# The last expert stored tile by tile, the final sum in the experts' block, and the first expert rows loaded inside the attention block

## The reference, cut to what matters

```python
x = x + 0.5 * ffn0(layernorm(x))      # 8 experts, top 2, capacity counted per expert
x = x + attention0(layernorm(x))      # 16 heads of 8, keys from a strided convolution
x = x + 0.5 * ffn0(layernorm(x))
x = x + 0.5 * ffn1(layernorm(x))      # causal attention inside, then 16 experts, top 2
x = x + attention1(layernorm(x))      # causal, 16 heads of 8
x = x + 0.5 * ffn1(layernorm(x))

# the experts of ffn1, after its own attention and layer norm (xt)
m1, m2 = one_hot(top1), one_hot(top2)           # of 16 experts
m1 = m1 * (loc1 < C); m2 = m2 * (loc2 < C)      # C = 512 rows an expert
xin  = einsum('tec,td->ecd', dispatch, xt)      # rows sent to the experts
h    = gelu(xin @ fc1_w + fc1_b)                # 128 -> 512
eout = (h @ fc2_w + fc2_b) * 0.8                # 512 -> 128
out  = resid + einsum('tec,ecd->td', combine, eout)
```

## Time and profile before

| | |
|---|---|
| median of 3 runs | 1950.85 us |
| lowest, highest | 1948.93, 1954.16 us |
| the profiled execution: its own time | 1948.95 us |
| its span, first to last instruction | 1947.2 us |
| PE busy | 1548.6 us (80%) |
| DVE busy | 1297.8 us (67%) |
| ACT busy | 966.4 us (50%) |
| POOL busy | 1078.7 us (55%) |
| mean granted clock of TensorE | 0.879 |
| HBM read, written | 104.34, 80.74 MB |

### The profile page before, as it was taken

How to read it: one execution, slowest core, us unless ns; L and a number is a source line. 1 busy time by engine, 2 the same in 40 slices (tenths; PEclk the granted TensorE clock), 3 DMA queues, 4 the chain that set the end, 5 groups by cost and what they waited for, 6 DMA issues and landing times. The chain is left out here.

```text
span 1947.2 us, 46256 instructions
## 1 busy us (share of the span) xinstructions
PE 1548.6 (80%) x17646; PEld 941.7 (48%) x17646; DVE 1297.8 (67%) x3322; ACT 966.4 (50%) x2039; POOL 1078.7 (55%) x1712
## 2 busy tenths in 40 slices
PE   5648788876599999854798599999999999744993
PEld 4532333345255555433576355555555555423772
DVE  7348888782688878734421688888888887544324
ACT  4215667732166677520233166777777776411331
POOL 3447766505378775545355376555757765552552
PEclk9977999977599999865799599999999999755996
DMA  8443322204333223100343442332323322001445
GB/s 288 112 131 104 90 82 80 75 23 123 114 120 104 82 88 99 42 28 23 114 138 98 138 126 84 92 100 78 113 84 98 97 81 83 26 23 56 141 130 156
DMA packets 233185, 188.08 MB, mean 97 GB/s; under 512 B 30044, under 2 KB 221368, under 8 KB 232326
## 3 DMA queue, kind: packets, MB, share of 16 engines
q1 hardware_dynamic: 222582, 166.36, 28.5%
q0 software_dynamic: 10240, 18.76, 2.9%
q10 hardware_dynamic: 144, 0.00, 0.0%
HBM read 104.34 MB, written 80.74 MB: 95 GB/s over the span
## 5 line engine op out<-in xcount | busy, mean ns | idle before, releaser
L1008 DVE TENSOR_REDUCE mx<-PS 128x2 f32<-128x512 f32 (+3 forms) x1408 | 784.2, 612 | 189.0 <-PE PS L648 137.5
L858 ACT ACTIVATE pt<-PS 128x512 f32<-128x512 f32 (+2 forms) x1408 | 667.6, 537 | 312.1 <-PE PS L648 227.6
L665 PE MATMUL PS<-ka,qa 52*128 52x256 bf16 (+3 forms) x2048 | 461.7, 305 | 65.2 <-DVE mx L1008 47.4
L781 PE MATMUL PS<-qa,ka 55*128 55x512 bf16 (+3 forms) x1792 | 459.7, 321 | 41.3 <-DMA qa<-nm 17.8
L725 PE MATMUL PS<-pt,vs 128*32 128x512 f32 (+3 forms) x3584 | 349.6, 481 | 2.3 <-issue 1.5
L648 PE MATMUL PS<-mask_q,identh 64*128 64x64 bf16 x3072 | 299.5, 193 | 1.5 <-issue 1.4
L648 PE MATMUL PS<-mask_k,identh 64*128 64x64 bf16 x3072 | 299.0, 192 | 0.9 <-issue 0.9
L781 PEld LDWEIGHTS PS<-qa,ka 55*128 55x128 bf16 x1792 | 166.9, 94 | 273.7 <-issue 119.3
L648 PEld LDWEIGHTS PS<-mask_k,identh 64*128 64x128 bf16 x3072 | 249.2, 97 | 51.7 <-issue 6.8
L648 PEld LDWEIGHTS PS<-mask_q,identh 64*128 64x128 bf16 x3072 | 252.4, 98 | 31.0 <-issue 8.9
L1161 POOL CAST nm<-nm 16x128 bf16<-16x128 f32 x128 | 36.2, 283 | 340.1 <-ACT nm L890 329.3
(11 more groups left out here) (249 smaller groups left out, 2333.4 us busy)
## 6 DMA issues: line engine op xcount, KB each, us to landing
pt<-in_f_w SPq DMA_DIRECT2D x96, 256.0 KB
qa<-q_parts SPq DMA_DIRECT2D x256, 96.0 KB, 2.3
ka<-k_parts SPq DMA_DIRECT2D x192, 96.0 KB, 2.3
q_parts<-parts SPq DMA_DIRECT2D x32, 384.0 KB, 3.4
k_parts<-parts SPq DMA_DIRECT2D x24, 384.0 KB, 2.6
xn<-y_rows SPq DMA_DIRECT2D x32, 256.0 KB, 3.2
hid<-y_rows SPq DMA_DIRECT2D x32, 256.0 KB, 3.7
q_parts<-parts SPq DMA_DIRECT2D x32, 256.0 KB, 3.2
```

The costliest lines, as they stand in the source:

```text
L665: mm = pe.matmul(PS[:, bank, i * n:(i + 1) * n], k.qa[rows, b % 2, g, h // 2, qb * P:(qb + 1) * P], k.ka[rows, b % 2, g, h // 2, 0:n], sta ...
L781: mm = pe.matmul(PS[:, bank, i * n:(i + 1) * n], k.ka[rows, b % 2, g, h // 2, kb * P:(kb + 1) * P], k.qa[rows, b % 2, g, h // 2, q0:S], st ...
L858: nc.scalar.activation(k.pt[:, u % 2, at[c]:at[c] + len(heads) * n], PS[:, SC_BANK + c % RING, 0:len(heads) * n], ACT.Exp, scale=SCORE_SCA ...
L1008: nc.vector.tensor_reduce(out, PS[:, MX_BANK + t % RING, 0:len(heads) * n] .rearrange("p (h n) -> p h n", n=n), AX.X, ALU.max).then_inc(s. ...
```

## The change

There are three parts. First, the last expert of every experts stage is done tile by tile: TensorE waits for all four activations, runs the chunks inside the tile loop with a PSUM bank for each tile, and signals after each tile; VectorE adds the bias tile by tile; POOL waits for each tile before it sends it. Second, the last `experts1` call is given the output: its own block goes on with all sixteen loads of results, the sum and the stores, and the separate last block is gone. Third, in the attention blocks whose rows are sent, SP waits at the end for the probabilities, the marks' sum and all sent rows, and then issues the loads of rows of experts 0 to 2 and of weights of experts 0 and 1, which before were the first thing that SP did in the experts' block. `AHEAD` (3, as before) becomes a constant, and `load_weights` and `load_rows` become functions outside `moe`.

```diff
--- before.py
+++ after.py
@@ -66,6 +66,7 @@
 ROOT_STEPS = ((0.703952253, 2.38924456), (0.5, 3.0))
 XT_BANK, H_BANK, Y_BANK = 0, 2, 6
 INV_BANK = 5
+AHEAD = 3
 FIRST_PHASES = ((0, 16), (16, 32))
 PHASES = ((0, 20), (20, 28), (28, 32))
 SENT_PHASES = ((0, 8), (8, 16), (16, 28), (28, 32))
@@ -1322,6 +1323,16 @@
             if not r.sent:
                 for i in range(B - 3, B):
                     store_rows(sp, k, i)
+            else:
+                sp.wait_ge(*s.pv_done.at(U))
+                sp.wait_ge(*s.inv_full.at(1))
+                sp.wait_ge(*s.first_sent.at(16 * NT))
+                for j, (first, end) in enumerate(r.phases):
+                    sp.wait_ge(*s.second_sent[j].at(16 * (end - first)))
+                for e in range(AHEAD):
+                    load_rows(sp, k, r, e)
+                    if e < 2:
+                        load_weights(sp, k, front, e)
 
     counts = {
         s.ln_step: k.entry_steps, s.pl_step: k.pool_steps, s.st_ready: len(ENTRY_GROUPS), s.mo_ready: NB - B, s.fm_ready: B - 2,
@@ -1343,7 +1354,22 @@
         signal.base += n
 
 
-def moe(nc, k, r, src, dst, gate_scale, renorm, src_scale):
+def load_weights(sp, k, w, e):
+
+    s, par = k.sig, e % 2
+    sp.dma_start(k.w1[:, par, :], w.w1[e * C:(e + 1) * C, :]).then_inc(s.w1_landed[par].h, 16)
+    sp.dma_start(k.w2[:, par, :, :], w.w2[e * FH:(e + 1) * FH, :].rearrange("(f p) c -> p f c", p=P))\
+        .then_inc(s.w2_landed[par].h, 16)
+
+
+def load_rows(sp, k, r, e):
+
+    ring, capacity = e % RING_E, r.w.capacity
+    sp.dma_start(k.xe[ring][:, :, :], k.xe_rows[e * capacity:(e + 1) * capacity, :]
+                 .rearrange("(t p) c -> p t c", p=P)).then_inc(k.sig.xe_loaded[ring].h, 16)
+
+
+def moe(nc, k, r, src, dst, gate_scale, renorm, src_scale, final=None):
 
 
     s, PS, w, E, capacity = k.sig, k.PS, r.w, r.E, r.w.capacity
@@ -1358,7 +1384,7 @@
 
         return ap.unsqueeze(2).to_broadcast([P, NT, E])
 
-    AHEAD = RING_E - 1
+    LAST_BANKS = (Y_BANK + (E - 1) % 2, XT_BANK, Y_BANK + E % 2, XT_BANK + 1)
     landed, landings = (s.xe_loaded, 16) if r.sent else (s.xe_landed, 16 * ST)
 
     with nc.Block() as block:
@@ -1399,12 +1425,27 @@
                                        k.w2[:, par, f, :], start=(f == 0 and t == 0), stop=(f == FC - 1 and t == ST - 1))
                 mm.then_inc(s.y_full.h, 1)
 
+            def last_output():
+
+                par = (E - 1) % 2
+                pe.wait_ge(*s.w2_landed[par].at(16 * PAIRS))
+                pe.wait_ge(*s.y_ready.at(E - 2))
+                pe.wait_ge(*s.act_done.at(E * FC))
+                for t in range(ST):
+                    if t == 2:
+                        pe.wait_ge(*s.y_ready.at(E - 1))
+                    for f in range(FC):
+                        mm = pe.matmul(PS[:, LAST_BANKS[t], 0:C], k.hT[:, par, f, t * P:(t + 1) * P],
+                                       k.w2[:, par, f, :], start=(f == 0), stop=(f == FC - 1))
+                    mm.then_inc(s.y_full.h, 1)
+
             rows_T(0)
             for e in range(E):
                 hidden(e)
                 if e + 1 < E:
                     rows_T(e + 1)
-                output(e)
+                    output(e)
+            last_output()
 
         @block.scalar
         def _(act):
@@ -1489,6 +1530,14 @@
                 nc.vector.tensor_tensor(k.ys[ring][:, 0:ST, :], PS[:, Y_BANK + e % 2, 0:capacity]
                                         .rearrange("p (t c) -> p t c", c=C), b2, ALU.add).then_inc(s.y_ready.h, 1)
 
+            def last_result():
+                ring = (E - 1) % RING_E
+                dve.wait_ge(*s.y_stored[ring].at(16 * ST * (E // RING_E - 1)))
+                for t in range(ST):
+                    dve.wait_ge(*s.y_full.at(E + t))
+                    nc.vector.tensor_tensor(k.ys[ring][:, t, :], PS[:, LAST_BANKS[t], 0:C], w.b2[:, (E - 1) * C:E * C],
+                                            ALU.add).then_inc(s.y_ready.h, 1)
+
             differences()
             rows(0)
             shares()
@@ -1501,8 +1550,12 @@
                     gates()
                 elif src_scale and e <= NG:
                     scale_source(e - 1)
-            result(E - 1)
+            last_result()
             k.route_steps = link.n
+            if final is not None:
+                for i in range(B):
+                    for c in range(2):
+                        combine(nc, k, dve, dst, i, c)
 
 
 
@@ -1518,9 +1571,10 @@
 
             def deliver(e):
 
-                pool.wait_ge(*s.y_ready.at(e + 1))
                 for t in range(ST):
                     n = e * ST + t
+                    if t == 0 or e == E - 1:
+                        pool.wait_ge(*s.y_ready.at(e + 1 + t))
                     pool.indirect_dma_start(k.y_rows[:, :], bass.IndirectOffsetOnAxis(k.idx[:, 1, n:n + 1], 0),
                                             k.ys[e % RING_E][:, t, :], None).then_inc(s.y_stored[e % RING_E].h, 16)
 
@@ -1537,42 +1591,32 @@
 
         @block.sync
         def _(sp):
-            def load_weights(j, par):
-                e = 2 * j + par
-                if not (isinstance(j, int) and j < 1):
+            for e in range(E):
+                if e >= 2:
                     sp.wait_ge(*s.y_full.at(e - 1))
-                sp.dma_start(k.w1[:, par, :], w.w1[bass.ds(e * C, C), :]).then_inc(s.w1_landed[par].h, 16)
-                sp.dma_start(k.w2[:, par, :, :], w.w2[bass.ds(e * FH, FH), :].rearrange("(f p) c -> p f c", p=P))\
-                    .then_inc(s.w2_landed[par].h, 16)
-
-            def fetch_sent(e):
-                ring = e % RING_E
-                if e == 0:
-                    sp.wait_ge(*s.first_sent.at(0))
-                    for signal in s.second_sent:
-                        sp.wait_ge(*signal.at(0))
-                if e > AHEAD:
-                    sp.wait_ge(*s.eT_full.at(e - AHEAD))
-                sp.dma_start(k.xe[ring][:, :, :], k.xe_rows[e * capacity:(e + 1) * capacity, :]
-                             .rearrange("(t p) c -> p t c", p=P)).then_inc(s.xe_loaded[ring].h, 16)
-
-            if r.sent:
-                for e in range(AHEAD):
-                    fetch_sent(e)
-                    if e < 2:
-                        load_weights(e // 2, e % 2)
-            for e in range(E):
                 if not (r.sent and e < 2):
-                    load_weights(e // 2, e % 2)
+                    load_weights(sp, k, w, e)
                 if r.sent and e + AHEAD < E:
-                    fetch_sent(e + AHEAD)
+                    if e >= 1:
+                        sp.wait_ge(*s.eT_full.at(e))
+                    load_rows(sp, k, r, e + AHEAD)
             for ring in range(RING_E):
                 sp.wait_ge(*s.y_stored[ring].at(16 * ST * (E // RING_E)))
-            load_results(sp, k, 0)
+            if final is None:
+                load_results(sp, k, 0)
+            else:
+                out, stored = final
+                for i in range(B):
+                    load_results(sp, k, i)
+                for i in range(B):
+                    sp.wait_ge(*s.combined.at(2 * i + 2))
+                    sp.dma_start(out[i].rearrange("(t p) c -> p t c", p=P),
+                                 dst[:, i * S:(i + 1) * S].rearrange("p (t c) -> p t c", c=C)).then_inc(stored, 16)
+                sp.wait_ge(stored, 16 * B)
 
     counts = {
         s.diff_ready: 2, s.exp_ready: 2, s.rt_step: k.route_steps, s.eT_full: E, s.eT_free: E,
-        s.h_full: FC * E, s.act_done: FC * E, s.y_full: E, s.y_ready: E,
+        s.h_full: FC * E, s.act_done: FC * E, s.y_full: E + ST - 1, s.y_ready: E + ST - 1,
     }
     for group in (s.w1_landed, s.w2_landed):
         counts |= {x: 16 * PAIRS for x in group}
@@ -1967,8 +2011,8 @@
         def experts0(r):
             moe(nc, k, r, x, x, 0.5, ("add", 1e-9), 0.0)
 
-        def experts1(r):
-            moe(nc, k, r, hid, x, 0.5 * 0.8, ("max", 1.1920929e-07), 0.5)
+        def experts1(r, final=None):
+            moe(nc, k, r, hid, x, 0.5 * 0.8, ("max", 1.1920929e-07), 0.5, final)
 
         entry0 = Segment(attn0, x, x, False)
         entry1, entry1f = Segment(attn1, x, x, True), Segment(attn1f, x, hid, True, twice=True)
@@ -1980,24 +2024,7 @@
         attention(nc, k, [entry1f], route1)
         experts1(route1)
         attention(nc, k, [entry1, entry1f], route1)
-        experts1(route1)
-
-        with nc.Block() as block:
-            @block.vector
-            def _(dve):
-                for i in range(B):
-                    for c in range(2):
-                        combine(nc, k, dve, x, i, c)
-
-            @block.sync
-            def _(sp):
-                for i in range(1, B):
-                    load_results(sp, k, i)
-                for i in range(B):
-                    sp.wait_ge(*k.sig.combined.at(2 * i + 2))
-                    sp.dma_start(out[i].rearrange("(t p) c -> p t c", p=P),
```

(3 more changed lines are left out.)

## The result

The changed kernel takes 1940.06 us, median of 5 runs (1936.86 to 1941.49), against 1950.85 us (1948.93 to 1954.97, 5 runs) for the kernel before on the same chip: ratio 0.994 [0.992, 0.996], 10.8 us less. The profiled execution took 1940.06 us (span 1938.3, granted clock 0.884), 8.9 us less than the 1948.95 us profiled before.

The account below looks back on a forecast made before the run. It took the kernel to be bound by one core's dependent order, where all engines wait. Gains 0.8 + 4.7 + 1.95 + 3.9 = 11.35 us gave 1937.6 from the profile, 1939.5 from the median; forecast 1938.5, range 1934.5 to 1944.

Parts of the forecast that it names:

- early loads: Experts' entries of the third and fourth stages: rows loaded inside the attention block start TensorE 2.35 us earlier, 4.7 us together.
- final block: Final sum after the last sends: sixteen loads in a row, no barrier; gain 3.9 us, of which 1.95 is the tile order.
- tile order: Last expert of each stage: POOL sends earlier, 1.95 us per 512-row stage, 0.8 together for the 256-row stages.
- The clock keeps its time: Rival at the experts' entries: TensorE's clock rises at 1796.7 regardless, giving back 1.2 us each; 1940.9 us, chance 0.20.
- tile four is full at 1914.3 and added by 1914.6, well before POOL wants it: Last 512-row stage: tiles take TensorE 0.93 us each, so adds stay hidden behind POOL's 1.27 us a tile; gain 1.95 us.
- the price of the first tile: 256-row stages: first tile's matmuls start 0.1 us after the last activation and take 0.93; POOL sends 0.4 us earlier.
- The bound of 1.4 us for both short stages: Stages of 256 rows: tile order gains 0.8 us together, between 0 and 1.4, POOL's idle time there.
- the stall allowed for: Final sum: one added stall of 0.4 us, the second piece landing 2.6 us after the first against 2.24 of work.
- Pieces come slowly: Rival at the final sum: each piece lands 2.6 us after the last, 2.1 us back; 1940.6 us, chance 0.10.
- The rows are not there: Rival at the experts' entries: sends count as landed only with POOL's DRAIN; 6.8 us lost, 1945.3 us, chance 0.08.
- Slower: Rival at three attention entrances: low clock lasts 13 us longer, costing 6.5 us each; 1958 us, chance 0.03.
- The terms named for the range's lower end: Below the forecast: 0.8 barrier at its bound, 0.4 no stall, 1.0 profiled run's level, 1.6 earlier clock rise; to 1934.5.

Follow-up runs that it names:

- chip Z: Chip of the last four follow-up kernels: kernel before 1951.03 us, changed kernel run again word for word 1943.50 us, ratio 0.996.
- fillers: Changed kernel plus 14 unused f32 matmuls on TensorE, after the last sent rows land in the attention block, chip Z: 1940.96 us, ratio 0.995 to the kernel before.
- chip Y: Chip of three tile loop shapes and the changed kernel with four early issues (1858.49 us, ratio 0.994); kernel before 1867.93 us there.
- taking issues away: Changed kernel with four early load issues instead of seven, and chunk waits, chip Z: 1940.85 us, ratio 0.994 to the kernel before.
- X: Chip of the moved wait and of the three parts each run alone; kernel before 1949.29 us there.
- the moved wait: Changed kernel with TensorE's wait before the last expert's third tile moved ahead of the first, chip X: 1942.65 us, ratio 0.996 to the kernel before.
- three loop shapes: Changed kernel with tiles three and four alternating, a wait per hidden chunk, or one signal after tile four, chip Y: 1858.34, 1858.36 and 1868.72 us.
- chunk waits: Changed kernel with a wait per hidden chunk in the last expert, not one for all four: 1858.36 us on Y; with four early issues on Z, 1940.85.

## Why the prediction was right

The forecast was 1938.5 us, range 1934.5 to 1944.0; measured 1940.06, and 1943.50 on chip Z. Total and sign came out. The early loads and the final block did what they were forecast to do; the tile order, two terms of the sum, did not, so it is partly luck that the total is this close.

- **Early loads: 4.7 us forecast, right in place and size.** At the six entrances profiled without early loads the restart lies 6.65 to 6.88 us after the marks, mean 6.79; at the eight with all seven issues early and no fillers, outside chip Y, 4.09 to 4.74, mean 4.38. That is 2.41 us each, forecast 2.35. SP is last at the barrier by the DRAIN lines, and taking issues away moved the barrier by 0.54 and 0.64. SP's first load came 0.07 to 0.69 us after the marks (forecast 0.25). In the third stage SP's DRAIN ends only 0.17 us behind POOL's in the first profile, in the fourth 0.8. Alone the part gave 4.2 us.
- **"The clock keeps its time" (0.20): did not happen.** In the first profiles it seemed to: the third stage's clock rose 7.0 us after the restart instead of 4.9, and that entrance gave back 1.05 us; the fourth gained 0.32. But the stretch from first to second transposes is 6.96 to 8.40 us, mean 7.79, at the six unchanged entrances, and 7.52 to 8.01, mean 7.71, at the ten early ones without fillers outside chip Y. What looked like a price was scatter. The rise itself came 4.9 to 7.8 us after the restart at the six, mean 6.5, and 6.0 to 7.0 at the ten, mean 6.4: it moved with the restart. The fillers show that it follows what TensorE does before. The Trainium skill (TensorE: Matmul & The Clock Gate, "What's actually happening") says that the monitor runs freely and that the moment of the transition therefore varies; it does not say that the rise keeps its time, which is what the rival needs. The scatter of the single entrances agrees with the page in kind.
- **Tile order: 4.7 us forecast (0.8 + 1.95 + 1.95), 1.3 came.** The step that failed is "tile four is full at 1914.3 and added by 1914.6, well before POOL wants it", worked out from 3.73 us for 32 matmuls. POOL's first send came 1.91 us earlier, as forecast (1.96), but the last only 0.59 in each 512-row stage: the third tile was added at +5.23, where its matmuls' modelled end is +3.06, and TensorE's DRAIN puts the end of the fourth 1.3 us behind its modelled +3.95. On chip Y the step holds: last send at +5.73, 1.92 us before the +7.65 of the earlier trace rows (the old loop has no profile from Y; on X it ends at +7.64). The short stages gained 0.07 and 0.10 instead of 0.4 each. There the price of the first tile failed: it was added 1.38 us after the activation, forecast 0.1 + 0.93 = 1.03, and that takes 0.35 of the 0.43 us. A tile by itself is not a quarter of the row: its eight records in the trace begin at +0.15 and end, by the model, at +1.28. The add took 0.29 us, as estimated (0.3). The bound of 1.4 us for both short stages is the idle time of one; two would have 2.8, and nothing hangs on it.
- **Final block: 1.95 us of its own forecast, 2.5 in the profile, 1.3 by the runs of it alone.** Over the seven profiles outside chip Y that have the block (last send to end of sum 23.82 to 25.40, mean 24.5) and the three that don't (25.85 to 26.58, mean 26.3) it is 1.8. The start, 5.94 us after the last send, is made of 2.31 to SP's first load, 0.41 to the second's issue and 3.22 for it to land; forecast 3.4. Eight pieces took 17.9 us, as forecast, without the stall allowed for. The other six of the seven profiles do have one stall, of 0.2 to 1.4 us; the mean over the seven is 0.5, forecast 0.4. "Pieces come slowly" (0.10) did not happen.
- **"The rows are not there" (0.08)** did not happen: in the fourth stage SP loads 3.0 us ahead of the end of POOL's DRAIN. On chip Y the rows are late, but because the sends are: SP loads 2.2 us after the start of the last send and some 4 us before POOL's DRAIN ends. **"Slower"** did not happen.

Put together with these sizes: 0.2 + 1.2 + 4.8 + 1.8 = 8.0 us, against 11.35 forecast. Measured are 10.8 us in the first measurement (by the interval 8.6 to 15.2), 7.5 on chip Z (4.9 to 10.9) and 6.6 on X with the moved wait (5.1 to 11.5). So the forecast came close to the first measurement although 3.4 us of its tile order were not there; 1.1 us in unchanged code and the scatter of the medians stand in their place. That is luck: with 8.0 us the kernel would take 1942.9, inside the range, but 4.4 us from the forecast. The terms named for the range's lower end add up to 3.8 us, which gives 1934.7, not 1934.5. What holds TensorE up in the tile loop on X and Z and not on Y stays open: no row shows a releaser.

## What to carry to other kernels

At a barrier list every engine's DRAIN end. The latest holds the block, and its distance to the second latest is all that a cut there can bring (here SP, then POOL's 5.3 us tail; with fillers TensorE itself). A row of matmuls has no measured end; where a consumer depends on a tile in its midst, price the tile by an add or a DRAIN that waited for it. A single entrance moved by 1.4 us between profiles of one code, so judge a clock effect of that size over several entrances. And test a timing theory beside the unedited kernel on a chip that shows the effect: three loop shapes looked like cures only because the chip was another.

## What the runs showed of the hardware

- Chips differ by 4%, as far as one measurement on each can tell: the kernel before took 1949.29, 1867.93 and 1951.03 us, with a mean granted clock of 0.877, 0.898 and 0.878. TensorE's unexplained pauses before two lines of the attention (L782 and L726) were 17.3 us in the kernel before and 18.0 in the changed one at first, and none on chip Y, and there the order of late engines at the entrances was different too (POOL's sends end 8 to 12 us after the marks instead of before them).
- With the tile loop, in stages of 512 rows and outside chip Y only, the add of the third tile came 1.4 to 2.3 us later than on Y, and TensorE's DRAIN took 3.5 to 4.2 us instead of 2.2; with chunk waits the third add came 1.6 us later, the fourth 3.5, and the DRAIN took 5.7 to 5.8 us. The old loop shows none of this.
- At all eight entrances profiled on chip Y TensorE restarted 6.53 to 6.55 us after the start of POOL's last indirect send. POOL's DRAIN ended 5.3 us after that send's end, there and at the other entrances.
- 14 f32 matmuls of 128x128 that feed nothing, 4 to 5 us of TensorE, ended the low clock before the experts' block began and shortened the way from the first to the second expert's transposes from 7.5 to 7.9 us to 5.1. Idle times of 3.7 to 17.7 us ahead of the restart made no difference to it.
